# Products of ones before the first weights, and two turns of X moved, in an eight-block transformer kernel

## The reference

```python
x = _layernorm(x + _L0_attn_ref(x, ...))   # lightning attention, 16 heads of 16, chunks of 128, rms norm
x = _layernorm(x + _L0_ffn_ref(x, ...))    # binarized 256 x 256
x = _layernorm(x + _L1_attn_ref(x, ...))   # multi-query causal attention
x = _layernorm(x + _L1_ffn_ref(x, ...))    # gated, with Hadamard transforms
x = _layernorm(x + _L2_attn_ref(x, ...))   # gated cumulative sum and a convolution
x = _layernorm(x + _L2_ffn_ref(x, ...))    # up 256 -> 1024, squared relu, rms norm, down; ternary weights
x = _layernorm(x + _L3_attn_ref(x, ...))   # 16 heads of 128, rotary, window of 64, with a sink
x = _layernorm(x + _L3_ffn_ref(x, ...))    # silu-gated, dequantized weights
```

## Time and profile before

| | |
|---|---|
| median of 3 runs | 1589.44 us (1588.42 to 1589.71) |
| the profiled execution | 1589.51 us, span 1587.7 us |
| PE busy | 1509.0 us, 95% of the span |
| DVE, ACT, POOL busy | 1033.7, 780.5, 362.7 us |
| mean granted clock | 0.99 |

### The profile page before, as it was taken

The page is one execution under the profiler, slowest core; times in us unless marked ns, Lnnn a source line. Parts: engine busy times, 40 slices in busy tenths (PEclk is TensorE's granted clock), DMA queues, the critical chain, the costliest instruction groups (busy, mean ns, idle before and its releaser), DMA issues.

```text
span 1587.7 us, 35631 instructions
## 1 busy us (share of the span) xinstructions
PE 1509.0 (95%) x14908; PEld 944.1 (59%) x14908; DVE 1033.7 (65%) x1866; ACT 780.5 (49%) x1801; POOL 362.7 (23%) x404
## 2 busy tenths in 40 slices
PE   7999889999999999899999989999999999999998
PEld 4667455444444444445666647777777777764556
DVE  4678678888898875624436965367787778842223
ACT  2431447777768887231111254377767677641110
POOL 2322000001000004100000044344555555630000
PEclk9999889999999999999999999999999999999999
DMA  6000231000000003100000040000000020000000
GB/s 195 2 2 8 80 87 21 13 10 10 14 3 14 3 13 116 61 2 19 1 0 0 1 133 1 7 1 8 1 8 1 1 91 1 2 0 1 14 14 27
DMA packets 31822, 39.05 MB, mean 25 GB/s; under 512 B 7531, under 2 KB 26606, under 8 KB 31150
## 3 DMA queue, kind: packets, MB, share of 16 engines
q1 hardware_dynamic: 31662, 36.77, 8.0%
HBM read 23.79 MB, written 2.10 MB: 16 GB/s over the span
## 4 chain that ended last, share of the span: by engine, by line
PE 80%; DVE 12%; ACT 3%; issue 3%; POOL 1%; DMA 0%; SPq 0%; POOLq 0%; ACTq 0%; DVEq 0%
PE PS L1264 7%; PE PS L1494 7%; PE PS L1500 7%; PE PS L1219 7%; PE PS L1523 7%; PE PS L2743 6%; PE PS L1250 6%; DVE arena L1403 4%; PE PS L2250 4%; PE PS L2730 3%; PE PS L2708 3%; PE PS L2573 2%; PE PS L340 2%; PE PS L2220 2%; PE PS L2589 2%
## 5 line engine op out<-in xcount | busy, mean ns | idle before, releaser
L1333 ACT ACTIVATE arena<-PS 128x512 f32<-128x512 f32 (+3 forms) x640 | 313.7, 534 | 119.7 <-PE PS L1254 57.5
L1403 DVE TENSOR_REDUCE arena<-PS 128x1 f32<-128x1024 f32 (+7 forms) x320 | 326.8, 1059 | 56.5 <-PE PS L1222 40.6
L1250 PE MATMUL PS<-arena 99*32 99x512 bf16 (+3 forms) x2560 | 210.8, 350 | 1.4 <-ACT arena L1333 1.0
L1219 PE MATMUL PS<-arena 96*32 96x512 bf16 (+3 forms) x2560 | 184.2, 356 | 18.1 <-DVE arena L1403 17.1
L1264 PE MATMUL PS<-arena 128*32 128x512 f32 (+3 forms) x1280 | 148.2, 536 | 2.2 <-ACT arena L1339 1.4
L191 POOL TENSOR_TENSOR rstd<-ve,mhalf 128x4 f32<-128x4 f32 x31 | 31.7, 1022 | 503.7 <-DVE ve L219 503.6
L2894 ACT ACTIVATE arena<-arena 128x128 f32<-128x128 f32 x256 | 122.7, 485 | 0.0
L1494 PE MATMUL PS<-XT,arena 128*128 128x512 f32 x256 | 120.4, 592 | 0.9 <-DVE arena L1731 0.9
L2743 PE MATMUL PS<-arena 128*128 128x256 f32 x512 | 121.0, 379 | 0.2
L1500 PE MATMUL PS<-XT,arena 128*128 128x512 f32 x256 | 120.3, 592 | 0.0
L1219 PEld LDWEIGHTS PS<-arena 96*32 96x32 bf16 x2560 | 64.1, 98 | 94.2 <-DVE arena L1403 42.8
(11 more groups left out here) (251 smaller groups left out, 2694.7 us busy)
## 6 DMA issues: line engine op xcount, KB each, us to landing
arena<-arena SPq DMA_DIRECT2D x79, 128.0 KB, 2.4
XT<-in_L_attn_xT SPq DMA_DIRECT2D x4, 512.0 KB, 7.4
X<-in_L_attn_x SPq DMA_DIRECT2D x4, 512.0 KB, 9.3
arena<-in_L_attn_out_w SPq DMA_DIRECT2D x1, 2048.0 KB, 8.2
out<-X SPq DMA_DIRECT2D x3, 512.0 KB, 3.0
arena<-in_dmask SPq DMA_DIRECT2D x1, 1024.0 KB, 5.7
arena<-in_L_ffn_W_up SPq DMA_DIRECT2D x1, 1024.0 KB, 5.1
arena<-in_L_ffn_W_gate SPq DMA_DIRECT2D x1, 1024.0 KB, 7.5
```

The lines of the kernel that those rows point to most:

```text
L1219: last = pe.matmul(flat[p, o:o + w], q[:, p], a.KS[0:SROWS, CH * kc:CH * kc + w], start=True, stop=kc < c)
L1250: last = pe.matmul(PS[p, b, lo:CH], keys[:, p], a.QS[0:rows, G1 * g + r, CH * c + lo:CH * (c + 1)], start=True, stop=j < TPC * c)
L1333: act.activation(a.PB[:, n % 3, r, lo:CH], PS[:, 4 + x % 3, lo:CH], ACT.Exp, scale=D0 ** -0.5).then_inc(a.e2, 1)
L1403: dve.tensor_reduce(dst, src, AX.X, ALU.max, negate=True).then_inc(a.m1, 1)
```

## The change

Four edits in three places. (1) `l0_pool` sets the ones first and signals `init` once there and once behind the last buffer; ACT, DVE and PE's first state product wait for both; PE waits for the first signal and does 22 products of ones by ones, 128 x 128 float32, into bank 3, before it comes to the first projection. (2) At the start of layer 2's feed-forward the last `tail_pe` of the attention moves from behind up-tile 3 to behind up-tile 4, and its `tail_act` from ahead of relu 2 to behind relu 5 and square 4 (and the middle part of chunk 2). (3) In the last attention the wait for XT moves from right behind the three turns of X to the next step, ahead of the turn of the queries and so behind that step's scores.

```diff
--- before.py
+++ after.py
@@ -244,6 +244,7 @@
 RING0 = 4
 L1_VX = 17408
 QK0, TURN0, V0, S0, O0 = 0, 1, 2, 3, 7
+WARM0, WARM_BANK = 22, S0
 SUMS0 = E + 64
 
 
@@ -374,7 +375,7 @@
             pe.wait_ge(a.kvup, t)
             pe.wait_ge(a.sq, t)
         else:
-            pe.wait_ge(a.init, 1)
+            pe.wait_ge(a.init, 2)
         O = PS[:, O0, 0:E].rearrange("p (h i) -> p h i", h=KT)
 
         def from_state(kt):
@@ -414,6 +415,10 @@
         pe.wait_ge(a.v_ev, min(t + 5, NT))
         pe.matmul(PS[:, V0, SUMS0 + t:SUMS0 + t + 1], a.SQs[:, t % 2, :], k.ones[:, 0:1], start=True, stop=True).then_inc(a.ssq, 1)
 
+
+    pe.wait_ge(a.init, 1)
+    for _ in range(WARM0):
+        pe.matmul(PS[:, WARM_BANK, 0:P], k.ones[:, :], k.ones[:, :], start=True, stop=True)
     for n in range(NT + 4):
         if 0 <= n - 2 < NT:
             scores(n - 2)
@@ -468,7 +473,7 @@
             act.wait_ge(a.sqs, t - 1)
         act.activation(a.SQ[:, t % 2, :, :], O, ACT.Square).then_inc(a.sq, 1)
 
-    act.wait_ge(a.init, 1)
+    act.wait_ge(a.init, 2)
     act.wait_ge(a.ld1, 16 * 6)
     for n in range(NT + 3):
         if n < NT:
@@ -484,8 +489,8 @@
 
 def l0_pool(k, pool, st):
     a = k.l0
+    pool.memset(k.ones[:, :], 1.0).then_inc(a.init, 1)
     pool.memset(k.mhalf[:, :], -0.5)
-    pool.memset(k.ones[:, :], 1.0)
     pool.memset(a.KV, 0.0)
     pool.memset(a.VM, 0.0).then_inc(a.init, 1)
     pool.wait_ge(a.ld1, 16 * 6)
@@ -566,7 +571,7 @@
                           ALU.add).then_inc(a.rs_v, 1)
 
     dve.wait_ge(a.ld1, 16 * 6)
-    dve.wait_ge(a.init, 1)
+    dve.wait_ge(a.init, 2)
     for n in range(NT + 3):
         if 0 <= n - 2 < NT:
             decay_scores(n - 2)
@@ -1898,10 +1903,9 @@
     pe.wait_ge(k.l2f.part, len(TERNARY_DVE))
     for it in range(EARLY2):
         l2f_up(k, pe, 0, it)
-    tail_pe(k, pe, NC * 6 - 1, NC - 1)
-
-
-EARLY2 = 4
+
+
+EARLY2, TURN2 = 4, 5
 
 
 def l2_hidden_act(k, act, c):
@@ -1953,7 +1957,6 @@
     x_middle(k, act, NC - 3)
     l2f_relu(k, act, 1)
     x_high(k, act, NC - 2)
-    tail_act(k, act, NC * 6 - 1, NC - 1)
 
 
 def l2_set(k, pool):
@@ -2261,6 +2264,8 @@
         last.then_inc(a.ssq, 1)
 
     for it in range(EARLY2, HT):
+        if it == TURN2:
+            tail_pe(k, pe, NC * 6 - 1, NC - 1)
         up(0, it)
     for c in range(NC):
         if c + 1 < NC:
@@ -2310,6 +2315,8 @@
                 square(c, it - 1)
             if (c, it) == (0, 4):
                 x_middle(k, act, NC - 2)
+            if (c, it) == (0, TURN2):
+                tail_act(k, act, NC * 6 - 1, NC - 1)
             if (c, it) == (0, 6):
                 act.wait_ge(k.xt_done, NC * 5)
                 x_high(k, act, NC - 1)
@@ -2758,6 +2765,8 @@
         if n < NG3:
             if g < 2 and t + 2 < NT:
                 project(t + 2, g)
+            if c >= 1 and (j, g) == (2, 2):
+                pe.wait_ge(k.xt_done, NC * 6 + c)
             if g >= 2 and t + 1 < NT:
                 turn(t + 1, g - 2)
         if 2 <= n <= NG3 + 1:
@@ -2778,7 +2787,6 @@
                 pe.wait_ge(a.b6, use6)
                 pe.wait_ge(a.b7, use7)
                 tail_pe(k, pe, NC * 7 + c - 1, c - 1)
-                pe.wait_ge(k.xt_done, NC * 6 + c)
     pe.wait_ge(k.l3f.w, L3F_PIECES + 4)
     for it in range(EARLY3):
         glu_up(k, pe, k.l3f, 7, 0, it)
```

## The result

The changed kernel takes 1583.13 us, the median of 7 executions (1582.62 to 1588.08), against 1589.44 (also 7) for the kernel before beside it; the ratio is 0.9971, 95% interval 0.9958 to 0.9984. That is 4.6 us, with an interval of 2.5 to 6.7. The ratio goes by all executions: their means, 1584.5 and 1589.1, lie 4.6 apart too, while the medians lie 6.3 apart, because four of the seven executions stand at 1582.6 to 1583.1 and three at 1585.0 to 1588.1.

A forecast was written before the change was run, and what follows sets the result against it. The prediction took TensorE to bound the kernel (80% of the chain), so only its idle or low-clock time could be won. 0.4 + 0.3 + 3.05 = 3.75 us off 1589.51 gave 1585.76, 1585.7 against the median; range 1583.9 to 1588.4.

The forecast's parts named there:

- Part 1: Start: 22 products of ones raise the clock for the first projection; gain 0.4 us (-0.3 to +0.8).
- Part 2: Layer 2's feed-forward start: square 3 comes 1.3 us earlier, about 1.0 given back; gain 0.3 us (-0.8 to 1.4).
- Part 3: Last attention: scores run during the copy to XT at three places; gain 3.05 us (1.0 to 3.3).
- Rival A: Last attention: the moved wait comes back at the keys, gain 1.0 instead of 3.05, total 1587.7; chance 10%.
- B: Start: the ones overrun and the clock does not rise; 3.6 lost, 3.35 won, total 1589.8; chance 6%.
- C: Layer 2's feed-forward start: the last turn pushed back costs more than it frees, -0.8, total 1586.9; chance 5%.
- D: Layer 2's feed-forward start: the clock falls in the thinned stretch, 6.6 to 7.8 us lost, total 1593.0; chance 6%.
- E: A clock fall, as at 896.89 (1.7 us lost), goes away since all work before it moves; total 1584.0; chance 7%.

The follow-up runs named there:

- kernel 10: The changed kernel, word for word, one execution for a second profile: 1580.22 us.
- kernel 1: The kernel before with only the 22 products of ones added: 1587.58 us, ratio 0.9991.
- 2: The kernel before with only the last turn of layer 2 moved: 1589.18 us, ratio 0.9997.
- 3: The kernel before with only the three waits for XT in the last attention moved behind the scores: 1586.73 us, ratio 0.9982.
- kernel 9: The kernel before, word for word, one execution for a second profile: 1584.73 us.
- kernel 4: The changed kernel with ScalarE's copy to XT and the high part moved behind up-tile (1,1)'s relu: 1583.45 us, ratio 0.9965.
- kernel 6: The changed kernel with 44 products of ones instead of 22: 1590.09 us, ratio 1.0005.
- kernel 5: The changed kernel with 14 products of ones instead of 22: 1583.22 us, ratio 0.9964.
- kernel 7: The changed kernel with 14 products of ones and the copy and high part moved behind up-tile (1,1)'s relu: 1581.85 us, ratio 0.9955.

## Why the prediction was right, point by point

**Part 1: mechanism right, size too small.** The forecast had the ones over at 8.4 and the clock up 5.0 us after they begin. In the profile of after they are over at 8.47 and the first recorded rise is at 6.20, 5.2 us after 0.98; the start gains 0.47, against 0.4 said. But that rise is not fixed: over the four profiles with 22 ones it came 3.6 to 5.3 us after the first product, the first projection at 7.69 (kernel 10) to 8.53 (kernel 1), and the gain was 1.26 to 0.42. The three profiles without ones (2, 3, 9) stand 0.13 to 0.38 behind the first of before, so that one had an early start. The mean of the four less the mean of all four without ones is 0.9 (-0.73 against +0.17). That is twice the 0.4 forecast and just over the term's upper bound of 0.8, mainly by the early rises: the forecast took a rise after 5.0 us out of bounds of 4.2 and 6.5, and the shortest was 3.6. The overrun was seen rightly as what eats the gain: 18 ones, which overrun nothing, give 1.57.

**Part 2: the chain was right, the sum 0.3 too small.** On the clock of before, with 2.9 added: POOL's first add ends at 922.4 (said 922.5), hidden tile 2 at 923.0 (923.05), the residual at 924.1 (924.2), POOL's second add at 925.3 (925.4), and square 3 begins at 925.8 (926.0), 1.5 us earlier than before instead of 1.3. That DVE and POOL take turns, on which the middle value of 0.3 rested, is in the rows above: hidden tile 2 is recorded with 1.76 us where alone such an operation takes 0.69, and ends 0.56 behind the end of POOL's add at 919.54. This is the rule of the Trainium skill, page "SBUF — State Buffer", section "SBUF: two separate sides" (an exclusive lock on the shared port pair, the loser waits for the whole instruction); the trace agrees with it here again. Of the 1.5 about 0.9 is given back to the copy, which stands behind square 4 in this stretch; kernel 4 takes it out, with the high part, and gets 0.99. So the given-back share agrees with what was said, and the term is off by the 0.2 of the chain and 0.1 of the copy. One test of the prediction came out wrong: PE's idle time ahead of up-tiles was to fall from 5.0 to about 4.5, and is 5.7 (six waits, the longest 2.29 ahead of up-tile 7, as said). I had left out of the account the idle time ahead of the transposes: before, PE waited 1.60 us there for the last normed X, and up-tile 4 now fills that. The two rows, of the timeline of before and of PE's waits of after:

```profile
919.52 1.09 PE L179 MATMUL PS<-ident,X 128*128 128x128 f32 x8 [1.60 <-DVE X L228]
```

```profile
PE PS L2223 <- ACT arena L2233: 5.7, 6, 2.3
```

The loads of the last attention, issued later, cost nothing: that stage shows only its own 3.1.

**Part 3: right in mechanism and size.** 3.12 to 3.17 in all eight profiles that have the edit (3.05 said). The three steps are 1.06, 1.07 and 1.01 in after. Rival A needed the keys' wait to grow from 0.77; it is 0.73.

**Rivals.** A and B are out, as is C (part 2 gains in every profile in which the clock holds). **D, a fall in the thinned start of layer 2's feed-forward, did happen**, in kernel 10, from 922.74 to 926.16, but at a price of 0.5 us and not 7.3: the stage gained 0.03 instead of 0.57. Its stretches:

```profile
922.75:926.15 3.40, 3.28 (x9) 0.94 (x8) 1.16 (x2) 3.40 (x6) 2.16 (x2) 0.50 0.58 169
926.20:930.00 3.80, 3.80 (x19) 2.47 (x18) 2.40 (x3) 2.27 (x4) 2.99 (x2) 1.00 0.94 387
```

It lasted 3.4 us. At half clock that loses 1.7 us of work, and about 1.0 of it went into the two waits of 0.54 and 0.41 that PE has there otherwise. Kernel 6 had such a fall too, at 933.14 in the dense part, and its stage gained 0.31 instead of 0.57. The working of D had doubled five up-tiles and a stretch of the dense part; the step that failed is the length, for the row it could have used was the 3.40 at 896.89. In the kernel before the same kind of fall costs nothing (kernels 1, 3 and 9, stage 0 to -0.01), for there it is hidden in longer waits (those ahead of up-tiles are 3.5 us in kernel 1 and 3.9 in kernel 9, against 5.0). **E, a fall goes away,** is what the profile of after shows (two, 1.87 and 0.68), but E's reason, that all work before it moves, is not needed for it: kernel 9 shows it with nothing moved.

**The number.** The forecast was 1585.7 and the median 1583.13. The ratio gives 4.6 us; the parts measured one by one give, by their ratios, 1.4 + 0.5 + 2.9 = 4.8, and by the stages 0.9 + 0.57 + 3.13 = 4.6. The sum of 3.75 was short by about 0.5 in part 1 and 0.3 in part 2. The remaining 1.7 us between forecast and median go with the half-clock stretches: the four executions from 1582.6 to 1583.1, the median among them, have a granted clock of 0.993, the three longer ones 0.990 or 0.991. What stays open is what decides where the clock falls in an execution, and whether the change makes falls rarer; no run here varied that alone.

## What to carry to other kernels

A wait belongs ahead of the first instruction that would overwrite something, not behind the one that made the data: 3.1 of the 4.6 us came from moving one line past work that doesn't need it. Filler that warms the clock should end where the real data lands: against the first profile of before, 18 products gained 1.6 us at the start, 22 on average 0.7, and 44 lost 3.7. And where the clock rises and falls within a run, subtract two profiles stage by stage and take a second profile of the unchanged kernel, before a difference is put down to an edit.

## What was unexpected of the hardware

- Two executions of the same kernel before differed by 4.8 us: 2.31 between 187 and 230, 1.86 near 644, 0.69 near 897, each where the granted clock was at its lower level in one and not, or for a shorter time, in the other. One edit's gain of 0.57 can't be seen in a single pair of profiles unless it is looked for in its own stage.
- The fall at 12.17 in kernel 5 came right after the ones had brought the clock up, behind idle times of 0.82 and 1.62 us, and was absent in kernel 7 with the same 14 ones and idle times of 1.25 and 1.58. So these idle times do not explain it, and no run here shows what does.
- The clock's record holds 1.00 until its first entry. Before that the 128 x 128 passes were 0.213 us apart, and 0.112 once it had risen, so the spacing of the passes, and not the column, tells the clock at the start.
